# Two batches' router and the first weight splits in the projection's block, and VectorE instead of GpSimd for the last two normalisations

## The chip, the cores and the metric

One Trainium2 chip, one of its cores. The metric is the device time of one execution in microseconds (us), the median of several executions. Of the kernel before three are known: 793.04, 795.33 and 796.99 us, median 795.33 us.

## What is computed

Four blocks on x of 4 batches x 512 tokens x 256 features, all in float32, each with a layer norm ahead and a gated residual behind it:

```
x = x + tanh(g_xattn[0]) * attention(layernorm(x), ctx)      # 16 heads of 16, rotary, then @ Wp.T + bp
x = x + tanh(g_ffn[0])   * experts(layernorm(x))             # 8 experts, top 2, and a shared one
x = x + tanh(g_xattn[1]) * coattention(layernorm(x), ctx)
x = x + tanh(g_ffn[1])   * bitlinear_ffn(layernorm(x))
```

The expert block takes logits = xn @ gate_w.T + lb_bias, sigmoid scores, the two highest of eight per token, and one mean weight per expert over all tokens (so a routed expert's output needs the scores of all four batches). Each expert, and each half of the shared one, is silu(xn @ gw.T) * (xn @ uw.T) @ dw.T with 128 inner features.

## The kernel before, in words

Each phase is a function with a program of its own for each engine, in an order written out by hand. Engines meet at semaphores only, and all of them at the end of each phase. The phases are prepare (QKV), attend, project, experts, coattend and bitffn. Two of them are touched.

**Project** (`phase_project`). SyncE issues the load of Wp (L680) and then, from the list `loads` (L682), the experts' down and up weights and the later phases' context. For each batch b, in four groups of heads, ScalarE copies the attention sums to `stage` (L688), TensorE transposes them (`sums`, L718), VectorE divides by the softmax sums (`normalise`, L767 and L769). TensorE transposes the result (`transposes`, L726), ScalarE copies that (L693), TensorE multiplies by Wp (`project`, L737), and VectorE adds to x and takes the row statistics (`residual`, L780 and L786). TensorE's order is sums(b), project(b-1), transposes(b); VectorE's is normalise(b), residual(b-1). All but the first batches run in hardware loops (`Fori`). GpSimd normalises batches 0 to 2 for the experts (`normalise_batch`: `batch_statistics`, nine small operations from L172 to L184, then two passes over four tiles, L194 and L198).

**Experts** (`phase_experts`). GpSimd normalises batch 3. TensorE transposes the normalised rows of each batch (L882, 8 transposes), ScalarE copies them to `xT_all` (`keep`, L1002), and TensorE makes the router's logits from them (`router`, L889, 2 matmuls, 4 in the trace). In the order of TensorE these steps stand among the first matmuls of the shared expert:

```python
transposes(0); transposes(1); router(0); transposes(2); router(1)
gate_up(0, 0); router(2); transposes(3); router(3)
# transposes of the logits (L954), gate_up(0, 1), project(0, 0)
# transposes of the selection (L965), project(0, 1), gate_up(0, 2) ...
```

A matmul of the experts is the sum of three, of operands split in a high part (ScalarE rounds it: `high_w` L1010, `high_d` L1014, `high_x` L1006, `high_h` L1022) and the rest (VectorE subtracts: `low_w` L1097, `low_d` L1102, `low_x` L1107, `low_h` L1091). `gate_up(c, k)` is 12 matmuls (L902) for chunk c and expert k of the order, and a 13th for a routed expert, which adds a large negative number where a token has not chosen it; `project(c, k)` is 6 matmuls (L915 to L920). Between them ScalarE applies the silu (L1018) and VectorE multiplies (`hidden`, L1085). VectorE ranks the scores (L1156 to L1161); only then can TensorE transpose the selection (L965), and VectorE copies it (L1170).

Of the kernel before, what the change touches and what calls it, by code (L numbers as in the profile page):

```python
# [19 lines left out]
F32 = mybir.dt.float32  # L20
# [8 lines left out]
P = 128  # L29
# [172 lines left out]
def phase_prepare(nc, a, per, qs, ks, va):  # L202
# [4 lines left out]
    with ExitStack() as ctx:  # L207
        sb = lambda n, s, d: ctx.enter_context(nc.sbuf_tensor(n, s, d))
        ps = lambda n, s, d: ctx.enter_context(nc.psum_tensor(n, s, d))
        sem = lambda n: ctx.enter_context(nc.semaphore(n))  # L210
# [197 lines left out]
        def _(pe):  # L408
# [40 lines left out]
            schedule(pe, step)  # L449

# [12 lines left out]
def phase_attend(nc, a, per, qs, ks, va, o32):  # L463
    id32 = per["c32"][:, C_ID:C_ID + P]
    with ExitStack() as ctx:
# [189 lines left out]
def phase_project(nc, a, per, norm, qs, loads):  # L655
    x_sb, st = per["x"], per["st"]
    id32 = per["c32"][:, C_ID:C_ID + P]

    o32 = qs[:, :, :].rearrange("p h s -> p (h s)").bitcast(F32).rearrange("p (s c) -> p s c", s=STEPS)
    with ExitStack() as ctx:  # L660
# [11 lines left out]
        ps_y = [ps(f"ps_y{i}", [P, 2, D], F32) for i in range(2)]  # L672
        wp_in, staged, t_done, r_done, on_done = (sem("wp_in"), sem("staged"), sem("t_done"),
                                                         sem("r_done"), sem("on_done"))
        oT_done, oT_ready, y_done, y_used = sem("oT_done"), sem("oT_ready"), sem("y_done"), sem("y_used")
        block = ctx.enter_context(nc.Block())

        @block.sync
        def _(sp):
            sp.dma_start(wp[:, :, :], a["wp"]).then_inc(wp_in, 16)  # L680
            for dst, src, arrived in loads:
                sp.dma_start(dst, src).then_inc(arrived, 16)  # L682

        @block.scalar
        def _(act):
            def stage_sums(s, u):
                wait(act, t_done, s - 1)
                act.copy(stage[:, u, :], o32[:, ds(s, 1), 0:S].rearrange("p o c -> p (o c)")).then_inc(staged, 1)  # L688
# [6 lines left out]
            for g in range(NG):  # L695
                stage_sums(g, g % 2)
            stage_sums(NG, 0)
            stage_sums(NG + 1, 1)
            transposed(0)
            with act.Fori(1, B - 1) as b:  # L700
                stage_sums(b * NG + 2, 0)
                stage_sums(b * NG + 3, 1)
                stage_sums(b * NG + 4, 0)
                stage_sums(b * NG + 5, 1)
                transposed(b)
            stage_sums(STEPS - 2, 0)
            stage_sums(STEPS - 1, 1)
            transposed(B - 1)

        @block.tensor  # L710
        def _(pe):
            def sums(b, g):

                s = b * NG + g
                pe.wait_ge(staged, s + 1)
                wait(pe, on_done, s - 1)
                for qt in range(QT):
                    last = pe.transpose(ps_t[g % 2][:, qt, :, :].rearrange("p j c -> p (j c)"),  # L718
                                        stage[:, g % 2, qt * P:(qt + 1) * P], id32)
                last.then_inc(t_done, 1)  # L720
# [10 lines left out]
            def project(b):  # L731

                pe.wait_ge(oT_ready, b + 1)
                for qt in range(QT):
# [7 lines left out]
            for g in range(NG):  # L742
                sums(0, g)
            transposes(0)
            for g in range(NG):
                sums(1, g)
            project(0)
            transposes(1)
            with pe.Fori(2, B) as b:
                for g in range(NG):  # L750
                    sums(b, g)
                project(b - 1)
                transposes(b)
            project(B - 1)

        @block.gpsimd
        def _(pool):
            for b in range(B - 1):
                normalise_batch(pool, per, norm, b)

        @block.vector
        def _(dve):
            def normalise(b, g):
                s = b * NG + g
                dve.wait_ge(t_done, s + 1)
                wait(dve, on_done, s - NG + 1)
                dve.reciprocal(recip[:, g, :, :], ps_t[g % 2][:, :, :, HD]).then_inc(r_done, 1)  # L767
                dve.wait_ge(r_done, s + 1)
                dve.tensor_tensor(on[:, :, g * G * HD:(g + 1) * G * HD].rearrange("p q (j d) -> p q j d", d=HD),  # L769
                                  ps_t[g % 2][:, :, :, 0:HD],  # L770
                                  recip[:, g, :, :].rearrange("p q (j o) -> p q j o", o=1)
                                  .broadcast_to([P, QT, G, HD]), ALU.mult).then_inc(on_done, 1)

            def residual(b):
                for h in range(2):
                    k = b * 2 + h
                    dve.wait_ge(y_done, k + 1)
                    for q in range(2):
                        xs = x_sb[:, ds(b * QT + 2 * h + q, 1), :].rearrange("p o d -> p (o d)")
                        last = dve.scalar_tensor_tensor(out=xs, in0=ps_y[h][:, q, :],  # L780
                                                        scalar=coef[:, ds(b * QT + 2 * h + q, 1)],
                                                        in1=xs, op0=ALU.mult, op1=ALU.add)
                    last.then_inc(y_used, 1)
                    dve.wait_ge(y_used, k + 1)
                    for q in range(2):
                        dve.bn_stats(st[:, ds(b * QT + 2 * h + q, 1), :].rearrange("p o d -> p (o d)"),  # L786
                                     x_sb[:, ds(b * QT + 2 * h + q, 1), :].rearrange("p o d -> p (o d)"))\
                           .then_inc(norm["stats_done"], 1)
            for g in range(NG):
                normalise(0, g)  # L790
# [1156 lines left out]
```

## Time and profile before

| | |
|---|---|
| the profiled execution, its own time | 795.87 us |
| its span, first to last instruction | 794.0 us |
| busy in the span: TensorE / VectorE / ScalarE / GpSimd | 689.2 / 473.1 / 358.8 / 283.2 us |
| mean granted TensorE clock | 0.933 of full speed |
| attend ends, project begins | 307.9, 308.2 us |
| project ends, experts begins | 347.1, 347.5 us |

PE is TensorE's matmul (PEld its weight load), DVE VectorE, ACT ScalarE, POOL GpSimd, SP SyncE. A row of the timeline gives the start and the duration in us, the engine, the line, the operation, what it writes and reads and how often in a row, and in brackets the idle time before it and what ended that. A group of instructions gives count, busy us, mean ns of one, and the idle time before them.

### The profile page before, as it was taken

Reading aid. Unit: us, or ns where it says so; the run is one execution under the profiler, and the core shown is the slowest. Engines: PE = TensorE matmul, PEld = TensorE weight load, DVE = VectorE, ACT = ScalarE, POOL = GpSimd, SP = SyncE. Lnnn points to the kernel's source line nnn. Section 1 sums busy time; section 2 is a strip of 40 time slices with the busy share of each in tenths; the row PEclk is TensorE's granted clock in tenths of the full one; section 3 lists DMA queues with packets and bytes.
Section 4 is the critical chain, followed back from the end, with each engine's and each line's share of the span. In section 5 each row is a group of like instructions: output and inputs, shape, how many; then the busy total and the mean of one; then the engine's idle time right before and its main releaser. Section 6 shows DMA issues by size and latency. Waiting matters only on the chain. (4 is left out here: it accounts for less than half of the span.)

```text
span 794.0 us, 10607 instructions
## 1 busy us (share of the span) xinstructions
PE 689.2 (87%) x3503; PEld 441.0 (56%) x3522; DVE 473.1 (60%) x852; ACT 358.8 (45%) x644; POOL 283.2 (36%) x462
## 2 busy tenths in 40 slices
PE   3599959999999996878999999995699999966986
PEld 1277733433344333745777777774376776852554
DVE  3567658888888841746834343434355546447985
ACT  0156644888888886345432222431313031102665
POOL 1446523344433450580001010101040436246897
PEclk9799986999999999989999999998789899986999
DMA  6000000000000004800100000001100000000001
GB/s 195 14 27 26 20 8 0 1 1 1 1 1 1 1 1 164 314 15 0 70 37 1 1 0 0 1 0 43 25 1 0 1 1 0 1 0 2 26 33 47
DMA packets 14103, 21.43 MB, mean 27 GB/s; under 512 B 2161, under 2 KB 11505, under 8 KB 13297
## 3 DMA queue, kind: packets, MB, share of 16 engines
q1 hardware_dynamic: 13200, 20.34, 7.5%
q10 hardware_dynamic: 864, 0.59, 0.3%
q8 instruction: 23, 0.38, 0.2%
q14 instruction: 16, 0.12, 0.1%
HBM read 18.83 MB, written 2.10 MB: 26 GB/s over the span
## 5 line engine op out<-in xcount | busy, mean ns | idle before, releaser
L562 DVE TENSOR_REDUCE mx<-ps_f 128x2 f32<-128x1024 f32 x128 | 151.5, 1220 | 31.6 <-PE ps_f L500 31.3
L638 ACT ACTIVATE prob<-ps_s 128x512 f32<-128x512 f32 x256 | 134.6, 608 | 34.5 <-PE ps_s L518 34.5
L518 PE MATMUL ps_s<-q_stacks,k_stacks 64*128 64x512 f32 x256 | 90.2, 484 | 5.9 <-ACT prob L638 3.5
L518 PEld LDWEIGHTS ps_s<-q_stacks,k_stacks 64*128 64x128 f32 x256 | 35.8, 188 | 87.2 <-ACT prob L638 70.9
L500 PE MATMUL ps_f<-k_stacks,q_stacks 64*128 64x512 f32 x256 | 63.8, 449 | 6.8 <-DVE mx L562 5.3
L527 PE MATMUL ps_o<-prob,vst 128*32 128x512 f32 x512 | 69.0, 612 | 0.0
L1018 ACT ACTIVATE qs<-ps_g 128x512 f32<-128x512 f32 x40 | 23.9, 598 | 88.6 <-PE ps_u L902 88.6
L1085 DVE SCALAR_TENSOR_TENSOR h<-ps_u,most,qs 128x512 f32<-128x512 f32 x32 | 24.0, 751 | 62.5 <-ACT qs L1018 62.5
L589 POOL TENSOR_TENSOR q_stacks<-minus,q_stacks 128x1024 fp32r<-128x1024 f32 x16 | 38.0, 2372 | 55.0 <-ACT minus L629 55.0
L172 POOL TENSOR_TENSOR norm_tmp_att<-st 128x4 f32<-128x4 f32 x4 | 1.0, 240 | 142.4 <-DVE st L1124 142.4
L1527 ACT ACTIVATE qs<-ps_SC,nmax 128x512 f32<-128x512 f32 x16 | 11.0, 686 | 76.4 <-DVE nmax L1415 76.4
L1091 DVE TENSOR_TENSOR h_low<-h,h_high 128x512 fp32r<-128x512 f32 x40 | 27.6, 691 | 23.4 <-ACT h_high L1022 23.2
L1022 ACT CAST h_high<-h 128x512 fp32r<-128x512 f32 x40 | 24.8, 621 | 31.2 <-DVE h L1085 31.2
L500 PEld LDWEIGHTS ps_f<-k_stacks,q_stacks 64*128 64x128 f32 x256 | 30.8, 197 | 14.2 <-DVE mx L562 11.7
L393 POOL TENSOR_TENSOR qkr<-qkb,c 128x512 f32<-128x512 f32 x16 | 20.3, 1268 | 42.5 <-DVE stack L312 30.1
L1299 PE MATMUL ps_SC<-ks 128*128 128x512 f32 x64 | 31.8, 644 | 3.3 <-DVE ks L1409 2.3
L347 ACT CAST stack<-qkr 128x512 fp32r<-128x512 f32 x16 | 9.9, 618 | 54.0 <-DVE qkr L303 30.8
L430 PE MATMUL ps_kv<-wkv,ctxT 128*128 128x512 f32 x64 | 34.3, 663 | 0.0
L415 PE MATMUL ps_st<-c,stack 128*128 128x128 f32 x256 | 30.8, 274 | 3.9 <-ACT q_stacks L355 3.9
L1317 PE MATMUL ps_q<-ks,qs 128*128 128x256 f32 x128 | 30.9, 384 | 1.5 <-DVE hq L1444 1.5
L415 PEld LDWEIGHTS ps_st<-c,stack 128*128 128x128 f32 x256 | 28.7, 142 | 6.3 <-DVE stack L312 2.3
L916 PE MATMUL ps_yE<-h_high,down_low 128*128 128x512 f32 x80 | 32.1, 402 | 0.0
(278 smaller groups left out, 1524.2 us busy)
## 6 DMA issues: line engine op xcount, KB each, us to landing
up<-in_up SPq DMA_DIRECT2D x10, 256.0 KB, 6.7
x<-in_x SPq DMA_DIRECT2D x4, 512.0 KB, 8.0
ctxT<-in_ctxT SPq DMA_DIRECT2D x16, 128.0 KB, 2.1
ks<-in_ctxTC SPq DMA_DIRECT2D x1, 2048.0 KB, 13.3
ks<-in_ctx SPq DMA_DIRECT2D x1, 2048.0 KB, 18.8
out<-x SPq DMA_DIRECT2D x16, 128.0 KB, 1.7
down<-in_down SPq DMA_DIRECT2D x1, 1280.0 KB, 5.5
ks<-in_wqv SPq DMA_DIRECT2D x1, 1024.0 KB, 20.7
```

Of the source, the lines that this page charges most:

```text
L415: last = pe.transpose(ps_st[i][:, p, :], stack[:, u, i // 2, 2 * pair:2 * pair + 2, :] .rearrange("p h r -> p (h r)"), id32)
L430: last = pe.matmul(ps_kv[u][:, :, :], ctxT[:, u, c, :], wkv[:, c, :, :], start=(c == 0), stop=(c == DC - 1))
L500: last = pe.matmul(ps_f[n % 2][:, h, :], qs[rows(h), 2 * f + pair, qt * P:(qt + 1) * P], ks[rows(h), 2 * f + pair, :], start=True, stop=True)
L518: pe.matmul(ps_s[n % 3][:, :], ks[rows(h), 2 * s + pair, kt * P:(kt + 1) * P], qs[rows(h), 2 * s + pair, :], start=True, stop=True).then_i ...
L527: last = pe.matmul(ps_o[HPAD * j:HPAD * (j + 1), :], vst[:, s % 2, kt, HPAD * j:HPAD * (j + 1)], prob[:, kt % 2, j, :], start=(kt == 0), s ...
L562: dve.tensor_reduce(mx[:, f % 2, qt, 2 * pair:2 * pair + 2], ps_f[n % 2][:, :, :], AX_X, ALU.max).then_inc(used, 1)
L589: pool.tensor_tensor(own, minus[:, :, :].broadcast_to([P, 2, S]), own.bitcast(F32), ALU.add)\
L638: act.activation(prob[:, kt % 2, j, :], ps_s[n % 3][:, :], ACT.Exp, scale=SCALE)\
L916: pe.matmul(ps_y[half][:, :], down_low[:, e, own], h_high[:, u, :], start=False, stop=False)
L1091: dve.tensor_tensor(h_low[:, u, :], h32[:, u, :], h_high[:, u, :].bitcast(F32), ALU.subtract)\
L1299: last = pe.matmul(ps_S[q % 2][:, :], sT[:, c, q * P:(q + 1) * P], ctxT[:, c, ds(b * S, S)], start=(c == 0), stop=(c == DC - 1))
L1317: last = pe.matmul(ps_q[:, :], attT[:, q % 2, k, :], ctok[:, ds(b * QT + k, 1), :], start=(k == 0), stop=(k == QT - 1))
```

## The change

The PE, ACT and DVE loops of the projection are written out. In the projection's block, TensorE now also makes the router's logits of batches 0 and 1, the first of them between sums(3) and project(2), the second at the end, with one PSUM tile `ps_T` for the transposes. ScalarE and VectorE split the shared expert's weights in the loop over the batches, VectorE splits chunk 0 of x, normalises batch 2 itself (`normalise_late`, one pass of four tiles) and copies the first half of the logits. GpSimd takes only the statistics of batches 2 and 3. In the experts' block VectorE normalises batch 3, and the steps are reordered. gate_w is loaded by SyncE between Wp and the list `loads`. SyncE clears the first phase's semaphores in the attend phase, since more of them are needed now. The core of the diff:

```diff
@@ attend, SyncE
             sp.dma_start(bp[:, :], a["bp"].to_broadcast([P, D])).then_inc(bp_in, 16)
+            for done in spent:
+                sp.sem_clear(done)
@@ project, SyncE
             sp.dma_start(wp[:, :, :], a["wp"]).then_inc(wp_in, 16)
+            sp.wait_ge(gw_clear, 1)
+            sp.dma_start(gw[:, :, 0:E], a["gate_w"]).then_inc(gw_in, 16)
@@ project, ScalarE (was: the same order in a Fori, without the splits and keeps)
+            for s in range(NG + 2):
+                stage_sums(s)
+            for b in range(B - 1):
                 transposed(b)
+                for s in range(b * NG + 6, min(b * NG + 10, STEPS)):
+                    stage_sums(s)
+                if b == 1:
+                    act.wait_ge(pre["up_in"], 16 * (NX + 1))
+                    pre["high_w"](act, 0)
+                    pre["high_w"](act, 1)
+                    pre["high_d"](act, E, NX)
+            keep(0)
+            keep(1)
             transposed(B - 1)
+            pre["high_x"](act, 0)
+            for k in range(2, 4):
+                pre["high_w"](act, k)
+            keep(2)
+            keep(3)
@@ project, TensorE
+            def router(b):
+                pe.wait_ge(norm["normed"], b + 1)
+                for i in range(2):
+                    wait(pe, kept, 2 * b + i)
+                    for q in range(2):
+                        for c in range(DC):
+                            last = pe.transpose(ps_T[:, c, q * P:(q + 1) * P],
+                                                norm["tile"](b * QT + 2 * i + q)[:, c * P:(c + 1) * P], id32)
+                    last.then_inc(xT_done, 1)
+                if b == 0:
+                    pe.wait_ge(gw_in, 16)
+                pe.wait_ge(kept, 2 * b + 2)
+                for c in range(DC):
+                    last = pe.matmul(ps_lgT[HPAD * b:HPAD * (b + 1), :], gw[:, c, :], xT_all[:, c, b * S:(b + 1) * S],
+                                     start=(c == 0), stop=(c == DC - 1))
+                last.then_inc(lgT_done, 1)
+            sums(2)
+            project(1)
+            transposes(2)
+            sums(3)
+            router(0)
+            project(2)
+            transposes(3)
+            project(3)
+            router(1)
@@ project, GpSimd
-            for b in range(B - 1):
+            pool.memset(gw[:, :, :], 0.0).then_inc(gw_clear, 1)
+            for b in range(2):
                 normalise_batch(pool, per, norm, b)
+            for b in range(2, B):
+                batch_statistics(pool, per, norm, b)
@@ project, VectorE
+            normalise(0)
+            for b in range(1, B):
+                normalise(b)
                 residual(b - 1)
+                if b == 2:
+                    pre["low_w"](dve, 0)
+                    pre["low_w"](dve, 1)
+                    pre["low_d"](dve, 0, E, NX)
             residual(B - 1)
+            pre["low_x"](dve, 0)
+            normalise_late(dve, per, norm, 2, pre["late"])
+            dve.wait_ge(lgT_done, 2)
+            dve.tensor_copy(lgT[0:2 * HPAD, :], ps_lgT[0:2 * HPAD, :])
+def normalise_late(dve, per, norm, b, done):
+    x_sb, tmp = per["x"], norm["tmp"]
+    dve.wait_ge(norm["steps"], 5 * (b + 1))
+    for t in range(b * QT, (b + 1) * QT):
+        last = dve.tensor_scalar(norm["tile"](t), x_sb[:, t, :], tmp[:, 4, t:t + 1], tmp[:, 8, t:t + 1], ALU.add, ALU.mult)
+    last.then_inc(done, 1)
@@ experts, GpSimd: the memset of gw and normalise_batch(3) are gone
@@ experts, TensorE
-            transposes(0); router(0) ... (the order shown above)
+            pe.wait_ge(pre["late"], 1)
             transposes(2)
             pe.wait_ge(xsplit, 1)
+            pe.wait_ge(wsplit, 2)
+            gate_up(0, 0, (0,))
+            pe.wait_ge(pre["late"], 2)
+            transposes(3)
             router(2)
+            router(3)
+            gate_up(0, 0, (1,))
             pe.wait_ge(lgT_copied, 1)
...
             gate_up(0, 1)
             pe.wait_ge(nsel_ready, 1)
...
+            pe.wait_ge(lg_copied, 1)
+            pe.wait_ge(dsplit, 1)
+            project(0, 0)
             project(0, 1)
@@ experts, ScalarE
+            for k in range(4, 2 * B):
                 keep(k)
             act.wait_ge(lg_copied, 1)
             act.activation(score[:, :, :], logits[:, :, :], ACT.Sigmoid).then_inc(score_done, 1)
+            silu(0, 0)
+            pre["high_d"](act, 0, E // 2)
             silu(0, 1)
+            pre["high_d"](act, E // 2, E)
+            high_h(0, 0)
             high_h(0, 1)
             for k in range(SH, NX):
                 silu(0, k)
-                if k + 4 < NX:
-                    high_w(k + 4)
+                if k + 2 < NX:
+                    pre["high_w"](act, k + 2)
@@ experts, VectorE
+            normalise_late(dve, per, norm, 3, pre["late"])
             dve.tensor_copy(tri[:, :, :], c32[:, C_TRI:C_TRI + E * E].rearrange("p (e f) -> p e f", f=E))
+            pre["low_w"](dve, 2)
             dve.wait_ge(lgT_done, B)
+            dve.tensor_copy(lgT[2 * HPAD:P, :], ps_lgT[2 * HPAD:P, :]).then_inc(lgT_copied, 1)
... (logits)
+            pre["low_w"](dve, 3)
... (ranks)
+            hidden(0, 0)
             link(dve.tensor_tensor(weight, score[:, :, :], chosen, ALU.mult))
             hidden(0, 1)
... (the copies of the transposed selection)
+            low_h(0, 0)
             low_h(0, 1)
... (the mean weights)
-            low_d(1, 0, E // 2)
-            low_d(2, E // 2, E)
-            low_w(SH + 1)
+            pre["low_d"](dve, 1, 0, E // 2)
+            pre["low_d"](dve, 2, E // 2, E)
...
             for k in range(SH, NX):
                 hidden(0, k)
-                if k + 3 < NX:
-                    low_w(k + 3)
+                if k + 2 < NX:
+                    pre["low_w"](dve, k + 2)
```

## Rows read from the trace of the kernel before

**Rows 1.** Stretches: us, busy (count) of each engine, TensorE's granted clock, DMA share, GB/s
```profile
346.00:350.00 4.00, 2.52 (x11) 2.26 (x12) 0.80 (x2) 1.74 (x3) 3.37 (x14) 0.50 0.15 43
350.00:354.00 4.00, 4.00 (x14) 1.67 (x14) 2.78 (x3) 3.10 (x6) 3.88 (x4) 0.70 0.12 30
...
370.00:374.00 4.00, 1.90 (x15) 1.43 (x15) 3.80 (x7) 1.57 (x4) 0.00 (x0) 0.86 0.00 0
374.00:378.00 4.00, 4.00 (x19) 3.23 (x16) 3.46 (x9) 0.30 (x1) 0.00 (x0) 0.72 0.00 0
```

**Rows 2.** Timeline, the end of the projection and the start of the experts
```profile
340.35 0.20 POOL L172 TENSOR_TENSOR norm_tmp_moe<-st 128x4 f32<-128x4 f32 x1 [0.84 <-DVE st L786]
...
342.17 1.04 POOL L184 TENSOR_TENSOR norm_tmp_moe<-norm_tmp_moe,norm_power_moe 128x4 f32<-128x4 f32 x1
...
345.30 1.84 POOL L198 TENSOR_SCALAR qs<-qs,norm_tmp_moe 128x256 f32<-128x256 f32 x4
...
347.49 3.79 PE L882 MATMUL ps_xE<-c,qs 128*128 128x128 f32 x16 [3.98 <-PEq L660]
```

**Rows 3.** Timeline, VectorE: residual of batches 0, 1 and 3, and what follows
```profile
321.09 0.88 DVE L780 SCALAR_TENSOR_TENSOR x<-ps_y,coef,x 128x256 f32 x2 [1.09 <-PE ps_y L737]
...
324.98 0.26 DVE L767 RECIPROCAL recip<-ps_t 128x16 f32<-128x16 f32 x1
...
329.01 0.88 DVE L780 SCALAR_TENSOR_TENSOR x<-ps_y,coef,x 128x256 f32 x2 [1.07 <-PE ps_y L737]
...
332.62 0.26 DVE L767 RECIPROCAL recip<-ps_t 128x16 f32<-128x16 f32 x1
...
341.82 0.88 DVE L780 SCALAR_TENSOR_TENSOR x<-ps_y,coef,x 128x256 f32<-128x256 f32 x2 [1.55 <-PE ps_y L737]
...
344.45 0.75 DVE L786 BATCH_NORM_STATS2 st<-x 128x6 f32<-128x256 f32 x2
```

**Rows 4.** Timeline, TensorE's project(2) and project(3), and ScalarE between stages
```profile
331.02 1.07 ACT L693 COPY onT<-ps_oT 128x512 f32<-128x512 f32 x2 [3.18 <-PE ps_oT L726]
...
334.57 3.62 PE L737 MATMUL ps_y<-wp,onT 128*128 128x256 f32 x16
...
339.79 3.72 PE L737 MATMUL ps_y<-wp,onT 128*128 128x256 f32 x16 [0.73 <-ACT onT L693]
```

**Rows 5.** The page's DMA issues: KB each, median us from issue to landing
```profile
up<-in_up SPq DMA_DIRECT2D x10, 256.0 KB, 6.7
```

**Rows 6.** Group by shape, VectorE's splits of weights in the experts' phase
```profile
L1097 DVE TENSOR_TENSOR up_low<-up,w_high 128x512 fp32r<-128x512 f32 x8 | 5.5, 682 | 0.0
```

**Rows 7.** Timeline, the last batch's transposes and router, and the logits' transposes
```profile
361.27 1.09 PE L882 MATMUL ps_xE<-c,qs 128*128 128x128 f32 x8
...
361.96 1.07 ACT L1002 COPY qs<-ps_xE 128x512 f32<-128x512 f32 x2 [1.32 <-PE ps_xE L882]
...
363.09 1.90 PE L889 MATMUL ps_yE<-qs,gw 128*32 128x512 f32 x4 [0.73 <-ACT qs L1002]
...
365.11 0.69 DVE L1145 COPY qs<-ps_yE 128x512 f32<-128x512 f32 x1 [0.83 <-PE ps_yE L889]
...
365.85 0.66 PE L954 MATMUL ps_yE<-c,qs 128*128 128x128 f32 x4 [0.86 <-DVE qs L1145]
```

**Rows 8.** Single lines: ns min/median/max of one, first and last start
```profile
L280 DVE TENSOR_SCALAR xn<-x,meanA,rstdA x16: 404/406/1306, 10.0 to 88.1; 128x256 f32 x10, 128x256 f32<-128x256 f32 x6
...
L194 POOL TENSOR_SCALAR qs<-x,norm_tmp_moe x16: 473/478/1422, 328.1 to 354.3; 128x256 f32<-128x256 f32 x16
```

**Rows 9.** Timeline, from the selection's transposes to gate_up(0, 3)
```profile
372.80 1.88 PE L965 MATMUL ps_xE<-c,qs 128*128 128x128 bf16 x16 [2.10 <-DVE qs L1161]
...
375.01 1.28 DVE L1170 COPY nselT<-ps_xE 128x1024 bf16<-128x1024 bf16 x2
...
376.75 0.62 PE L902 MATMUL ps_g<-x_high,w_high 128*128 128x512 f32 x2
...
380.87 0.70 PE L902 MATMUL ps_g<-x_high,w_high 128*128 128x512 f32 x2 [0.84 <-DVE up_low L1097]
```

More of the change, by code:

```diff
@@ L741, in _ @@
             pe.wait_ge(wp_in, 16)
-            for g in range(NG):
-                sums(0, g)
+            sums(0)
             transposes(0)
-            for g in range(NG):
-                sums(1, g)
+            sums(1)
             project(0)
             transposes(1)
[L749 to L754, printed above, removed]
+            sums(2)
+            project(1)
@@ L762, in _, with normalise @@
         def _(dve):
[L763 to L772, printed above, removed]
+            def normalise(b):
+                for g in range(NG):
+                    s = b * NG + g
+                    dve.wait_ge(t_done, s + 1)
+                    wait(dve, on_done, s - NG + 1)
+                    if g == 0:
+                        wait(dve, oT_done, 2 * b)
+                    dve.reciprocal(recip[:, g, :, :], ps_t[g % 2][:, :, :, HD]).then_inc(r_done, 1)
+                    dve.wait_ge(r_done, s + 1)
+                    dve.tensor_tensor(on[:, :, g * G * HD:(g + 1) * G * HD].rearrange("p q (j d) -> p q j d", d=HD),
+                                      ps_t[g % 2][:, :, :, 0:HD],
+                                      recip[:, g, :, :].rearrange("p q (j o) -> p q j o", o=1)
+                                      .broadcast_to([P, QT, G, HD]), ALU.mult).then_inc(on_done, 1)
@@ L785, in residual @@
                     for q in range(2):
[L786 to L790, printed above, removed]
-            with dve.Fori(1, B) as b:
-                for g in range(NG):
-                    normalise(b, g)
+                        t = b * QT + 2 * h + q
@@ L801, in phase_experts @@
+def phase_experts(nc, a, per, norm, next_norm, pre, sg, h32, h_low, h_high, spare, nselT, up_low, down_low, w32, wabs,
+                  w32_in, abs_done):
     x_sb, c32, c16 = per["x"], per["c32"], per["c16"]
@@ L891, in router, with gate_up @@
                 last.then_inc(lgT_done, 1)
-            def gate_up(c, k):
+            def gate_up(c, k, halves=(0, 1)):
                 e, u = order[k], k % 2
@@ L898, in gate_up @@
                 terms = [(w, x, d) for w, x in terms for d in range(DC)]
-                for i, out in ((0, ps_g[u]), (1, ps_u[u])):
+                for i in halves:
+                    out = (ps_g[u], ps_u[u])[i]
                     masked = i == 0 and e < E
@@ L907, in gate_up @@
                         pe.matmul(out[:, :], skip[:, e, :], nselT[:, cols], start=False, stop=True)
-                last.then_inc(gu_done, 1)
+                if 1 in halves:
+                    last.then_inc(gu_done, 1)
             def project(c, k):
@@ L1171, in _ @@
                    .then_inc(nselT_ready, 1)
+            low_h(0, 0)
+            low_h(0, 1)
             link(dve.tensor_reduce(total[:, 0, :], weight, AX_X, ALU.add))
```

208 lines of the change are left out of this document (81 added, 127 removed).

## The prediction

> **What bounds the kernel now.** I read the table of engines first: TensorE is busy for 87% of the span, so time is lost only where it pauses or runs at its lower clock. The windows show where that is in the touched stretch: [rows 1] has the granted clock at 0.50 from 346 to 350 us and at 0.70 from 350 to 354, again below 1 from 370 to 378. The clock has two levels, 1.2 and 2.4 GHz, so 0.50 is the lower one throughout. Then the timeline gives the reasons. [rows 2]: TensorE has finished the projection at 343.5, but the block waits for GpSimd's normalisation of batch 2 until 347.14, and the experts begin at 347.49 on a slow array. Ahead of that, from 321 to 345 us, the projection is a ring: VectorE's residual, its normalise, TensorE's sums and project, the residual again [rows 3, 4]. Behind it the chain is TensorE, the ranks on VectorE, the selection's transposes at 372.80, and at 380.87 gate_up(0, 3) [rows 9]. From there TensorE has no pause of a whole microsecond, so what the change is worth is how much earlier gate_up(0, 3) starts.
>
> **The projection, step by step.** The sum is made against the profiled execution: 795.87 us, span 794.0, so 1.87 lie around it; it is 0.54 above the median of the runs.
>
> Loops written out: residual(0) and (1) last 3.89 and 3.61 us up to the next reciprocal, the unrolled residual(3) 344.45 + 0.75 - 341.82 = 3.38 [rows 3]. With 0.05 saved at each project ahead of them, both together bring 0.8: residual(1) ends at 331.8.
>
> New on VectorE there: two weight splits and one of down, all of 512 columns, 0.68 each [rows 6], 2.05 us in front of normalise(3), whose first operation starts at 333.9 instead of 332.62. Nothing hides them: sums(3) of the third group waits for it. ScalarE's halves (three copies, some 1.9 us) fit into its pause of 3.18 us [rows 4]; without it they would delay the copy for project(2). Their weights were issued by 314 us and land 6.7 us later [rows 5], ahead of their use at 327. The gate_w load moves `down` and `up` back by its own issue, some 0.5 us, with 6 us to spare, and Wp stands ahead of it. Clearing semaphores falls on SyncE, idle in attend: nothing.
>
> router(0) stands between sums(3) and project(2), in TensorE's own order. With one PSUM tile a half is 0.69 us from the first transpose to ScalarE's copy, 0.59 the copy, 0.06 back; twice that is 2.68, and the four matmul passes are 1.90 [rows 7]: 4.6 us, uncovered. GpSimd has normalised batch 0 before that. project(2) started 1.95 after normalise(3) began (334.57 - 332.62), so now at 333.9 + 1.95 + 4.6 = 340.45. project(3) follows 5.2 later [rows 4], at 345.65; residual(3) runs from 347.7 to 351.05; router(1) starts 3.6 after project(3), takes 4.6 and ends at 353.85; the copy of its logits 0.12 + 0.69 more [rows 7], to 354.7. Beside it VectorE has low_x(0) (1.36, two of [rows 6]) and four tiles of batch 2 at 0.41 [rows 8], done at 354.05. keep and high copies of ScalarE lie beside these.
>
> GpSimd's statistics of batch 3 take 2.86 us (340.35 to 342.17 + 1.04 [rows 2]), from 351.15 to 354.0, if nothing holds them. But VectorE subtracts and scales from SBUF at that very time, and rows show that each can hold the other: L280 took 1.306 instead of 0.406 us, L194 1.422 instead of 0.478 [rows 8]. Bounds of the delay: nothing, or low_x plus four tiles, 1.36 + 1.64 = 3.0, which would end the block at 357. The small operations have waits between them in which VectorE's can pass, so I take 1.5: statistics at 355.5, block at 355.5, 0.8 beyond 354.7. The Trainium skill (SBUF — State Buffer, SBUF: two separate sides) makes this an exclusive lock, in which the loser is held for the other's whole instruction. By that rule in full the sum would be 1.5 higher than mine; L194's row has such a hold of one operation.
>
> **The experts, step by step.** Begin at 355.5 + 0.3 = 355.8, 8.3 later than 347.49. Left for TensorE until the logits' transposes end: 1.1 transposes(2), 1.4 half of gate_up, 1.1 transposes(3), two routers 3.8, half of gate_up 1.4, 0.66 [rows 7]: 9.5, so 365.3 against 365.85 + 0.66 = 366.5 before: 1.2 gained. VectorE normalises batch 3 in 1.65, ready at 357.5, before TensorE asks at 358.3; its copy of the logits lies under the second half of gate_up.
>
> From there to gate_up(0, 3) it was 380.87 - 366.5 = 14.4. Now: low_w(3) stands before the ranks and is 0.68, where VectorE had a pause of 0.38 for the sigmoid: selection's transposes after 6.3 + 0.3 = 6.6, done at 8.5. project(0, 0) used to lie in the pause ahead of them and now lies behind. VectorE has hidden(0, 0), hidden(0, 1), 1.28 for the selection and low_h(0, 0) (2.75 us with the small ones) from 6.8 to 10.5; until then project(0, 0) can't end. Its last two passes 0.5, project(0, 1) 1.5, gate_up(0, 2) and the sums 3.3: 15.8. The wait of 0.84 for up_low [rows 9] is gone, since low_w(3) is done. That is 1.4 worse: the gain is given back, and gate_up(0, 3) starts at 381.1, 0.2 later than before. Later pairs of steps stay TensorE's.
>
> Clock: the new pause ahead of sums(3)'s third group is 2.8 us (331.8 to 334.6), and TensorE idles 3.6 instead of 2.1 us before the selection's transposes. After a pause of 2.1 us the rows have the low level for 0.14 x 2 x 4 + 0.28 x 2 x 4 = 3.4 us [rows 1], half of it lost. Bounds for each place: nothing, or 1.7; the cold start after 347.49 is gone in the step sum above. I take 0.5 in all, as much of the stretch waits for VectorE anyway.
>
> Sum: 0.2 + 0.5 on the execution's 795.87, that is 796.6, and on the median 795.33 + 0.7 = **796.0 us**.
>
> **Rivals.** (1) Slower, by the clock. Place: the splits in front of normalise(3). If the pause drops the array to 1.2 GHz as that at 343.5 did, where it stayed low for 4.0 + 2.4 = 6.4 us [rows 1], router(0) and project(2) lose up to 3.2, and the longer pause before the selection 1.7. 795.5 (the sum without a clock term) + 3.2 + 1.7 = 800.4. It decides from about 3 us of lower level in busy time. For it: 2.1 us were enough once; against it: the slices of the page show full clock through the projection's batches, which have pauses of 1 to 1.5 us. The Trainium skill (TensorE: Matmul & The Clock Gate, What's actually happening) has the array throttled by default and released by activity, which speaks against adding pauses. 0.18. (2) The hold between GpSimd and VectorE at its full 3.0 us: 796.0 + 1.5 = 797.5, still no change in a measurement. 0.14, where nothing else goes wrong. (3) Faster: VectorE's splits find slack in the ring, no hold, no low clock, and project(0, 0) overlaps the selection better: 795.5 - 2.05 - 0.8 (the hold) - 1.5 = 791.2. Against it: sums(3) waits for VectorE in every batch. 0.15. (4) The change doesn't do what it says: all orders are by hand, so nothing can put the steps elsewhere; no chance given.
>
> **Numbers.** No change as summed 0.53, with (2) 0.67; slower 0.18; faster 0.15. A measurement here tells apart about 0.5%, 4 us. The range from 791 to 800.5 takes in both ends of the unknown costs and leaves some 0.2 outside. The likeliest case alone is 793.5 to 798.5.
>
> **What would show it.** Right: the projection's block ends near 355.5 with GpSimd's statistics last, the logits' transposes end near 365, gate_up(0, 3) starts at 380 to 382, TensorE waits some 3.6 us for the selection. Wrong: router(0) costing well under 4.6, normalise(3) starting before 333, low clock from 334 to 341, or a start of gate_up(0, 3) outside 378 to 384.

## The result and the profile after

The median after is 797.22 us (793.07 to 799.08), beside 794.80 us (792.79 to 796.99) of the kernel before: a ratio of 1.003, 95% interval 1.0019 to 1.0042. That is 2.4 us slower and less than the 0.5% named ahead: no change in the sense of the forecast, 1.2 us above its number. The interval doesn't hold 1, though, so the small loss is real, and it is larger than the 0.7 us that the sum had forecast. The profiled execution took 798.58 us with a span of 796.8; the one before had 795.87 and 794.0.

The page of the kernel after, its totals of TensorE and the granted clock over 40 slices:

```profile
PE 692.7 (87%) x3503; PEld 443.0 (56%) x3522; DVE 475.9 (60%) x861; ACT 357.4 (45%) x643; POOL 276.3 (35%) x446
PEclk9699986999999999997999999998689899986999
```

The share of TensorE is still 87%. A page can't show where 2.4 us went, so I read the same stretch as before. Its measure in all that follows is the time from the issue of Wp, the first of the projection's block, to the start of gate_up(0, 3). Before, that is 308.15 to 380.87 = 72.72 us. After, it is 307.73 to 383.11 = 75.38, or 2.66 more. Outside the stretch the two traces differ by 0.14 us (308.15 + 413.13 before, 307.73 + 413.69 after). So near an agreement is partly chance: over the fourteen traces of this study the part ahead of the stretch takes 305.4 to 309.6 us and the part behind it 409.9 to 414.1, in code that the edits leave alone. The stretch itself repeats far better, 75.38 and 75.43 in two executions of the changed kernel.

The timeline of the kernel after, from residual(1)'s end to project(2) (start, duration, engine, line, operation, count, and in brackets the idle time ahead and what ended it), which answers to [rows 3, 4]:

```profile
330.92 1.28 DVE L876 TENSOR_TENSOR up_low<-up,w_high_shared 128x512 fp32r<-128x512 f32 x2
332.12 0.68 DVE L885 TENSOR_TENSOR down_low<-down,d_high_shared 128x512 fp32r<-128x512 f32 x1
332.72 0.25 DVE L815 RECIPROCAL recip<-ps_t 128x16 f32<-128x16 f32 x1
...
333.57 1.25 PE L741 MATMUL ps_t<-c,stage 128*128 128x128 f32 x8 [2.53 <-DVE on L817]
...
334.66 0.98 PE L772 MATMUL ps_TP<-c,qs 128*128 128x128 f32 x4
...
338.20 3.54 PE L779 MATMUL ps_lgTP<-qs,gw 128*32 128x512 f32 x4 [0.77 <-ACT qs L712]
...
341.67 3.72 PE L760 MATMUL ps_y<-wp,onT 128*128 128x256 f32 x16
```

The three splits stand between residual(1) and normalise(3), and TensorE's pause behind them is 2.53 us. Then router(0) runs from 334.66 to 341.67, 7.0 us instead of the 4.6 of the sum. Its four matmul passes take 3.54 us, and 1.90 for router(1) later in the same block: the lower of the two levels of TensorE's clock. The windows of the kernel after (first the stretch and its length, then each engine's busy time with its count, the granted clock, the DMA share and GB/s), which answer to [rows 1]:

```profile
334.00:338.00 4.00, 2.76 (x14) 1.79 (x12) 1.31 (x5) 1.11 (x2) 3.70 (x8) 0.59 0.07 27
338.00:342.00 4.00, 3.80 (x6) 0.84 (x7) 0.00 (x0) 0.06 (x1) 1.14 (x3) 0.56 0.02 4
342.00:346.00 4.00, 4.00 (x24) 3.57 (x22) 2.20 (x6) 0.14 (x1) 0.00 (x0) 1.00 0.00 0
...
358.00:362.00 4.00, 4.00 (x18) 3.39 (x16) 1.39 (x5) 1.24 (x3) 0.00 (x0) 0.58 0.24 67
...
374.00:378.00 4.00, 3.99 (x19) 2.98 (x17) 3.94 (x8) 1.24 (x2) 0.00 (x0) 0.50 0.00 0
378.00:382.00 4.00, 4.00 (x15) 3.02 (x16) 3.41 (x6) 0.00 (x0) 0.00 (x0) 0.86 0.01 4
```

There are three low stretches in these rows, and each follows a pause of TensorE: 2.53 us ahead of 334, 2.43 at the start of the experts, 3.63 ahead of the selection. Now the end of the projection's block, with GpSimd's statistics of batch 3 (the timeline of the kernel after, which answers to [rows 2]):

```profile
352.33 1.21 DVE L894 TENSOR_TENSOR x_low<-qs,x_high 128x1024 fp32r<-128x1024 f32 x1
352.56 1.03 POOL L172 TENSOR_TENSOR norm_tmp_moe<-st 128x4 f32<-128x4 f32 x1 [2.52 <-DVE st L834]
353.45 1.38 DVE L854 TENSOR_SCALAR qs<-x,norm_tmp_moe 128x256 f32<-128x256 f32 x4
...
355.10 0.68 DVE L847 COPY lgT<-ps_lgTP 64x512 f32<-64x512 f32 x1 [0.27 <-PE ps_lgTP L779]
...
355.74 1.04 POOL L184 TENSOR_TENSOR norm_tmp_moe<-norm_tmp_moe,norm_power_moe 128x4 f32<-128x4 f32 x1
...
357.49 1.07 PE L975 MATMUL ps_xE<-c,qs 128*128 128x128 f32 x8 [2.43 <-PEq L668]
```

The statistics last from 352.56 to 356.78, 4.2 us instead of 2.86 [rows 2]; the block waits for them, a whole microsecond after the copy of the logits, and the experts begin at 357.49. The rest of the chain in the same timeline, which answers to [rows 7, 9]:

```profile
366.42 0.60 PE L1043 MATMUL ps_yE<-c,lgT 128*128 128x128 f32 x4
...
373.43 1.89 PE L1050 MATMUL ps_xE<-c,qs 128*128 128x128 bf16 x16 [3.63 <-DVE qs L1202]
...
379.98 0.63 PE L996 MATMUL ps_g<-x_high,w_high 128*128 128x512 f32 x2
...
383.11 0.70 PE L996 MATMUL ps_g<-x_high,w_high 128*128 128x512 f32 x2
```

Cut at the start of the experts and at the end of the logits' transposes, the stretch is 39.34 + 19.02 + 14.36 = 72.72 us before and 49.76 + 9.53 + 16.09 = 75.38 after. The projection's part grew by 10.42, the experts' first part lost 9.49, and the part behind the logits grew by 1.73.

### The profile page after: what moved, and what is told of

Its sections match the earlier page's. It is cut to its first block and busy times, and to the rows that moved or that the text cites. A ratio compares the mean times of both kernels' runs of the same rounds, so it can differ in the third digit from the quotient of the medians.

```text
span 796.8 us, 10544 instructions
## 1 busy us (share of the span) xinstructions
PE 692.7 (87%) x3503; PEld 443.0 (56%) x3522; DVE 475.9 (60%) x861; ACT 357.4 (45%) x643; POOL 276.3 (35%) x446
## 5 line engine op out<-in xcount | busy, mean ns | idle before, releaser
L172 POOL TENSOR_TENSOR norm_tmp_att<-st 128x4 f32<-128x4 f32 x4 | 1.0, 241 | 144.6 <-DVE st L1169 144.6
```

## The experiments

Theory A, after the result: the splits' place costs their own 2.05 us and, through the pause, the lower clock in router(0), about 2.4 more. B: the clock has nothing to do with that pause, and router(0) is slow in this place for another reason. Later runs went after the hold of GpSimd, the order behind the logits, and the single parts of the change. The expectations compare with the kernel after unless they say otherwise. There are twelve runs, eleven new kernels and the change itself again. The last column is measured side by side with the kernel before and is not always the quotient of two medians:

| kernel | stretch, us | median, us (runs) | ratio to before, 95% |
|---|---|---|---|
| before | 72.72 | 794.80 (20) | |
| after | 75.38 | 797.22 (20) | 1.0030, 1.0019 to 1.0042 |
| e1, splits later | 70.73 | 791.86 (7) | 0.9951, 0.9935 to 0.9968 |
| e2, filled pause | 73.96 | 795.18 (12) | 0.9994, 0.9976 to 1.0011 |
| e3, router(0) at the end | 71.72 | 794.28 (10) | 0.9974, 0.9958 to 0.9990 |
| e4, loops alone | 71.58 | 792.85 (10) | 0.9945, 0.9923 to 0.9967 |
| e5, e1 and low_x ahead | 68.49 | 790.77 (4) | 0.9942, 0.9925 to 0.9958 |
| e6, e1 and filled rank pause | 68.62 | 791.68 (4) | 0.9949, 0.9931 to 0.9967 |
| e7, e1 and project ahead | 70.55 | 789.95 (4) | 0.9933, 0.9916 to 0.9950 |
| e8, normalisation alone | 74.88 | 796.57 (10) | 1.0017, 0.9995 to 1.0039 |
| e9, e5 and e7 | 67.90 | 787.25 (4) | 0.9911, 0.9877 to 0.9945 |
| e10, e9 and filler | 66.79 | 788.82 (4) | 0.9918, 0.9902 to 0.9935 |
| e11, e5 and filler | 67.72 | 789.16 (4) | 0.9920, 0.9900 to 0.9941 |
| e12, the change again | 75.43 | 797.21 (6) | 1.0025, 1.0012 to 1.0038 |

The ratio is to the runs of the kernel before on the same chip, whose median moved between 794.7 and 796.4.

A stretch is one execution's, and its sum hides where the clock was low. So it is cut here as above, at the start of the experts and at the end of the logits' transposes:

| kernel | projection | experts' first part | behind the logits |
|---|---|---|---|
| before | 39.34 | 19.02 | 14.36 |
| after | 49.76 | 9.53 | 16.09 |
| e12 | 49.82 | 9.53 | 16.08 |
| e1 | 45.45 | 7.99 | 17.29 |
| e2 | 47.29 | 9.58 | 17.09 |
| e3 | 47.52 | 7.99 | 16.21 |
| e4 | 37.69 | 19.53 | 14.36 |
| e5 | 44.30 | 7.99 | 16.20 |
| e6 | 45.40 | 8.00 | 15.22 |
| e7 | 46.48 | 9.52 | 14.55 |
| e8 | 40.91 | 19.61 | 14.36 |
| e9 | 44.51 | 7.99 | 15.40 |
| e10 | 44.26 | 7.99 | 14.54 |
| e11 | 44.52 | 7.99 | 15.21 |

In the kernels that have the change's order, the first part takes 8.0 us where the clock stays at 1.00 and 9.5 where it falls. No edit touches that part.

### The splits in another place (e1)

```diff
                 normalise(b)
-                residual(b - 1)
-                if b == 2:
+                if b == 3:
                     pre["low_w"](dve, 0)
                     pre["low_w"](dve, 1)
                     pre["low_d"](dve, 0, E, NX)
+                residual(b - 1)
```

> The changed kernel with the three splits of VectorE moved from ahead of normalise(3) to behind it, into the 8 us in which VectorE waits for project(2). Clock theory (the splits open a pause of 2.8 us on TensorE, after which it falls to 1.2 GHz and router(0) takes 7.0 instead of 4.6 us): both go, 2.05 + 2.4, project(2) starts 4.4 us earlier relative to the block's start and the median is about 793. Work theory (the slow router is not the pause's doing): only the 2.05 go, router(0) still takes about 7 us, about 795.

The timeline of e1, TensorE alone:

```profile
331.75 1.25 PE L741 MATMUL ps_t<-c,stage 128*128 128x128 f32 x8 [0.72 <-DVE on L817]
332.84 0.60 PE L772 MATMUL ps_TP<-c,qs 128*128 128x128 f32 x4
...
335.54 1.88 PE L779 MATMUL ps_lgTP<-qs,gw 128*32 128x512 f32 x4 [0.77 <-ACT qs L712]
337.35 3.72 PE L760 MATMUL ps_y<-wp,onT 128*128 128x256 f32 x16
...
353.14 1.06 PE L975 MATMUL ps_xE<-c,qs 128*128 128x128 f32 x8 [2.40 <-PEq L668]
```

With the pause at 0.72 us, router(0) takes 337.35 - 332.84 = 4.5 us, and project(2) starts 4.3 us earlier than in the kernel after, at the same issue of Wp within 0.04 us. 1.8 of these are the third group's earlier start, 2.5 the shorter router(0). The stretch falls by 4.65 us and the kernel becomes 0.5% faster than before. Only the 4.3 are the edit's: the experts' first part is 1.5 shorter, since behind the same pause (2.40 us) the clock stayed high this time, and the part behind the logits is 1.2 longer. Moving three operations of VectorE by one step of its ring is worth more than the whole change loses; that the 2.5 are the clock's, e1 alone can't show.

### The pause kept but filled (e2)

```diff
+                    if s == STEPS - 3:
+                        for i in range(18):
+                            pe.transpose(ps_T[:, i % 2, 0:P], id32, id32)
```

The transposes of a constant are work on top, between the second and the third group of sums(3); the splits stay where the change put them.

> The changed kernel with 18 more transposes of a constant on TensorE in the pause ahead of the third group of sums(3), some 2.4 us of work into an unused PSUM tile; nothing waits for them and all orders stay. Clock theory: the clock holds at 1.00 from 334 to 342, router(0) takes 4.6 us, about 2.4 us faster than the changed kernel, near 794.8. Work theory: no faster than the changed kernel, 797.

The timeline of e2, TensorE alone, and one of its windows:

```profile
329.89 2.13 PE L746 MATMUL ps_TP<-c 128*128 128x128 f32 x18
332.60 1.25 PE L741 MATMUL ps_t<-c,stage 128*128 128x128 f32 x8 [0.57 <-DVE on L820]
333.68 0.60 PE L775 MATMUL ps_TP<-c,qs 128*128 128x128 f32 x4
...
338.19 3.72 PE L763 MATMUL ps_y<-wp,onT 128*128 128x256 f32 x16
```
```profile
354.00:358.00 4.00, 4.00 (x16) 3.50 (x17) 1.91 (x6) 1.17 (x2) 0.00 (x0) 0.58 0.19 67
```

This settles it between A and B. The third group still starts where VectorE lets it, 332.60 - 306.68 = 25.9 us after the issue of Wp (after: 25.8), and router(0) takes 4.5 us instead of 7.0. So 2.5 us of the kernel after are the clock's alone, set off by the pause. Only 1.4 of them stay in the stretch: the experts start at the lower clock here as in the kernel after (0.58), and the part behind the logits is 1 us longer. The time agrees with the trace: 0.9994 of before against 1.0030 for the kernel after, with intervals apart, though this kernel does more work.

### Both routers behind project(3) (e3)

```diff
@@ TensorE
-            router(0)
             project(2)
...
             project(3)
+            router(0)
             router(1)
```

ScalarE's two copies for router(0) move behind its copy for project(3).

> The changed kernel with router(0) behind project(3), next to router(1), and ScalarE's two copies behind the copy for project(3). The same work on TensorE. If router(0) costs what it does because it stands in the ring, residual(3) comes 7 us earlier, GpSimd's statistics of batch 3 are done under the routers and the block ends about 1.7 us earlier: near 795.5. If the place doesn't matter, TensorE's sum is the same and only the hold of the statistics (1.1 us) goes: near 796.1.

The timeline of e3, TensorE alone:

```profile
333.04 1.25 PE L741 MATMUL ps_t<-c,stage 128*128 128x128 f32 x8 [2.53 <-DVE on L817]
334.13 5.30 PE L760 MATMUL ps_y<-wp,onT 128*128 128x256 f32 x16
```

The pause is the same 2.53 us, and now project(2) pays for it, 5.30 instead of 3.72 us. The stretch is 3.7 us shorter than after. 2.2 of them lie in the projection, for two reasons that this run doesn't part: the low clock costs 1.6 instead of 2.5, and router(0) lies beside the last residual and the statistics of batch 3 instead of in front of them. The other 1.5 are the experts' first part at the full clock, behind a pause of 1.17 us instead of 2.43.

### The parts of the change by themselves (e4, e8)

e4 is the kernel before with its three projection loops written out (TensorE's is shown, ScalarE's and VectorE's are alike):

```diff
-            with pe.Fori(2, B) as b:
+            for b in range(2, B):
```

> The kernel before with nothing but the projection's loops of TensorE, ScalarE and VectorE written out. By the step sum 0.8 us, 0.1% faster than before, near 794.0, to be seen in the trace as project(3) starting 30.9 instead of 31.6 us after the block's first instruction. If the unrolled code costs elsewhere (instruction loads): no gain or slower.

The stretch is 1.1 us shorter, against 0.8 in the sum. At project(3), where the expectation looked, it is 1.3: it starts 335.76 - 305.43 = 30.3 us after the issue of Wp, 31.6 before. The time is lower by more than that, 0.55% by the ratio and 3.6 us between the medians: in the profiled execution the issue of Wp itself came 2.7 us earlier, in phases that the edit does not touch. Why they ran faster stays open.

e8 is the kernel before with the other part alone: GpSimd makes the statistics of batches 2 and 3 in the projection's block, and VectorE scales them.

```diff
-            for b in range(B - 1):
+            for b in range(2):
                 normalise_batch(pool, per, norm, b)
+            for b in range(2, B):
+                batch_statistics(pool, per, norm, b)
... (VectorE's normalise_late(2) behind residual(3), its normalise_late(3) first in the experts)
```

> The kernel before with nothing but the normalisation of batches 2 and 3 by VectorE (one pass of four tiles each, statistics still on GpSimd, those of batch 3 in the projection's block). By the step sum the block ends about 0.5 us earlier or up to 1.5 later, as GpSimd's statistics of batch 3 run beside VectorE's four tiles, 345.2 + 2.9 to 4.2 against 347.1 before; TensorE did not wait for batch 3 later. So no gain, 0 to 2 us slower in the stretch. If the two slow passes of GpSimd bounded the experts' start, 1.5 us faster or more.

The timeline of e8:

```profile
343.33 0.22 POOL L172 TENSOR_TENSOR norm_tmp_moe<-st 128x4 f32<-128x4 f32 x1 [2.15 <-DVE st L796]
...
345.53 1.04 POOL L184 TENSOR_TENSOR norm_tmp_moe<-norm_tmp_moe,norm_power_moe 128x4 f32<-128x4 f32 x1
...
347.10 2.30 PE L892 MATMUL ps_xE<-c,qs 128*128 128x128 f32 x9 [5.62 <-PEq L668]
```

The experts begin 347.10 - 306.19 = 40.9 us after the issue of Wp, 1.6 later than before: the scaling left GpSimd, but the statistics of batch 3, 3.24 us behind the last residual, came into the block in its place. They can't start earlier, since they need that residual. The stretch is 2.2 us longer, 0.6 of it in the experts' first part. In time this part alone is worth nothing, 1.0017 with 1 inside the interval.

### The subtraction away from GpSimd's statistics (e5)

e1 and:

```diff
+            pre["low_x"](dve, 0)
             residual(B - 1)
-            pre["low_x"](dve, 0)
```

> The kernel of e1_splits_later with low_x(0) ahead of residual(3), in VectorE's pause for project(3), so that it no longer runs beside GpSimd's statistics of batch 3. Hold theory (an operation of GpSimd that reads SBUF waits for VectorE's whole subtraction: L172 took 1.04 instead of 0.20 us): the statistics take 0.8 to 1.0 us less than their 4.2, and the projection's block, which they end, is that much shorter. If the stretched rows are the profiler's and GpSimd is only slow: the 4.2 us stay and the block ends as in e1.

The timeline of e5, GpSimd alone:

```profile
349.95 0.23 POOL L172 TENSOR_TENSOR norm_tmp_moe<-st 128x4 f32<-128x4 f32 x1 [1.45 <-DVE st L834]
...
352.16 1.04 POOL L184 TENSOR_TENSOR norm_tmp_moe<-norm_tmp_moe,norm_power_moe 128x4 f32<-128x4 f32 x1
```

and TensorE's first row of the experts:

```profile
353.87 1.06 PE L975 MATMUL ps_xE<-c,qs 128*128 128x128 f32 x8 [1.43 <-PEq L668]
```

L172 takes 0.23 us here, and 1.03 in the kernel after beside low_x (1.04 in e1). The statistics take 3.25 us instead of 4.2, and the experts begin 353.87 - 309.57 = 44.30 us after the issue of Wp instead of e1's 45.45. So 1.0 of the 1.4 us by which the statistics were held came from that one subtraction; the other 0.4 also show in e8, whose statistics have only the four tiles of scaling beside them (3.24 us). The stretch is 2.2 us shorter than e1's, 1.1 of it behind the logits, where this edit changes nothing and e1 happened to be slow; the ratios, 0.9942 and 0.9951, lie inside each other's intervals and don't part the two kernels.

### The rank pause filled (e6)

e1 and 26 transposes of a constant behind gate_up(0, 1), again work on top:

```diff
+            for i in range(26):
+                pe.transpose(ps_x[0][:, i % 2, 0:P], id32, id32)
```

> The kernel of e1_splits_later with 26 more transposes of a constant on TensorE in its pause of 3.6 us before the selection's transposes. If the low clock behind that pause costs time: the clock stays at 1.00, the selection's transposes take 1.1 us and project(0, 0) and (0, 1) some 1.5 us less in all, and the matmul of the sums comes 1.0 to 1.5 us earlier. If VectorE's chain (copies of the selection, low_h) sets the pace there: under 0.5 us.

The timeline of e6, TensorE alone:

```profile
362.47 3.00 PE L1047 MATMUL ps_xE<-c 128*128 128x128 f32 x26
366.25 1.07 PE L1052 MATMUL ps_xE<-c,qs 128*128 128x128 bf16 x16 [0.78 <-DVE qs L1204]
...
369.97 0.73 PE L1015 MATMUL ps_yE<-h_low,d_high_shared 128*128 128x512 f32 x2 [0.90 <-DVE h_low L1154]
```

The granted clock is 1.00 from 314 to 382, and from the start of the logits' transposes to the sums' matmul it is 15.68 us instead of 17.75 in e1: 2.1 us less. Against e1, whose low stretch behind this pause was a long one, the filler looks worth too much; between e5 and e11, or e9 and e10 below, it is 1.0. Of a faster TensorE a part turns into a wait for VectorE's low_h, 0.90 us. In time it can't be told from e1 (0.9949 and 0.9951).

### project(0, 0) ahead of the selection again (e7)

e1 and, in short: TensorE makes the main passes of project(0, 0) ahead of its wait for the ranks, as the kernel before did, and VectorE and ScalarE bring hidden(0, 0) and high_h(0, 0) forward.

```diff
+            project(0, 0, (0,))
...
-            project(0, 0)
+            project(0, 0, (1,))
```

> The kernel of e1_splits_later with the first four matmuls of project(0, 0) in TensorE's pause before the selection's transposes, hidden(0, 0) among VectorE's rank operations and low_h(0, 0) right behind the selection. Theory that the change gives its gain back by having put project(0, 0) behind the selection: the matmul of the sums comes about 1.2 us earlier, although the selection is 0.7 us later. If the place of project(0, 0) doesn't matter: the same, or 0.7 later.

The timeline of e7, TensorE alone:

```profile
363.57 0.60 PE L1046 MATMUL ps_yE<-c,lgT 128*128 128x128 f32 x4
...
369.81 0.77 PE L1011 MATMUL ps_yE<-h_high,d_high_shared 128*128 128x512 f32 x1 [2.86 <-ACT h_high L1102]
...
378.46 0.29 PE L1065 MATMUL ps_xE<-sums,ones 128*128 128x16 f32 x2
```

From the logits' transposes to the sums it is 14.89 us, 2.9 less than in e1 and more than the 1.2 expected. Most of that isn't the order's: the windows from 370 to 378 have the clock at 0.64 and 1.00 here, and at 0.50 and 0.79 in e1. The order itself comes out of e9 and e10 below as 0.8. The stretch as a whole is only 0.2 shorter than e1's, since the clock was low twice where e1's was not: the block began at the lower level (0.50 from 314 to 318, where e1 had 0.97), 1.0 us, and the experts' start fell (0.73 and 0.85 from 354 to 362), 1.5 us. The ratio is 0.9933 to e1's 0.9951, and the intervals overlap.

### Together (e9, e10, e11) and the change again (e12)

e9 has the edits of e5 and e7, e10 adds 22 transposes of a constant behind gate_up(0, 1), e11 is e5 with the 26 of e6.

> The kernel of e1_splits_later with the edits of e5_low_x_earlier and e7_project_first together. If the two gains lie behind one another (0.9 us in the projection's block, 1.5 to 2.5 us from the logits' transposes on), gate_up(0, 3) starts 68 us after the first issue of the projection's block, against 70.7 in e1, and the time is 0.8% under the kernel before. If each only moves the other's wait: as e1 or e5.

> The kernel of e9_both_orders with 22 transposes of a constant on TensorE between gate_up(0, 1) and the first matmuls of project(0, 0). If what is left behind that pause is the low clock: the clock stays at 1.00 and gate_up(0, 3) starts another 0.5 to 1.0 us earlier. If it is VectorE's chain: no change.

> The kernel of e5_low_x_earlier with the filled pause of e6_filled_rank_pause, orders otherwise those of the change. Clock theory: 1 us or more under e5, near e10, since the low level behind that pause was worth as much as the order. Order theory: near e5, 1.5 us over e9.

> The changed kernel unaltered, on this chip and beside these runs. Both theories: 0.2 to 0.4% slower than the kernel before, low clock somewhere between sums(3) and project(2).

The timeline of e9, TensorE alone:

```profile
357.88 0.60 PE L1046 MATMUL ps_yE<-c,lgT 128*128 128x128 f32 x4
...
365.96 1.93 PE L1056 MATMUL ps_xE<-c,qs 128*128 128x128 bf16 x16
...
373.74 0.29 PE L1065 MATMUL ps_xE<-sums,ones 128*128 128x16 f32 x2
```

and that of e10:

```profile
359.69 0.60 PE L1046 MATMUL ps_yE<-c,lgT 128*128 128x128 f32 x4
...
362.91 2.56 PE L1050 MATMUL ps_xE<-c 128*128 128x128 f32 x22
...
374.59 0.29 PE L1067 MATMUL ps_xE<-sums,ones 128*128 128x16 f32 x2
```

e9 is the fastest kernel of the study by its median, 787.25 us, 0.9911 of before and below both kernels. Its transposes of the selection still run at the lower clock (1.93 us for 16; e6 has 1.07). e10 takes that away and its stretch is the shortest, 66.79, but its time can't be told from that of e9, nor can e11's. So the fillers of the rank pause have shown themselves in the trace and not beyond that.

These runs part the order from the clock. From the start of the logits' transposes to the sums' matmul it is:

| | without filler, clock low | with filler, clock at 1.00 |
|---|---|---|
| the change's order | e5: 16.66 | e11: 15.67 |
| project(0, 0) ahead | e9: 15.86 | e10: 14.90 |

The order is worth 0.8 us at either level of the clock, and the clock 1.0 us in either order. The expectation of e9 held (67.9 for 68 us, 0.9% under before), and so did the clock's side of that of e10 (1.1 us earlier). For e11 neither theory fits: its stretch is 0.8 under e5 and 0.9 over e10, as both the clock and the order count.

e12 is the change unaltered, to see whether its low stretches are its own. The timeline, TensorE alone:

```profile
333.75 1.29 PE L741 MATMUL ps_t<-c,stage 128*128 128x128 f32 x8 [2.52 <-DVE on L817]
334.84 1.06 PE L772 MATMUL ps_TP<-c,qs 128*128 128x128 f32 x4
...
338.46 3.46 PE L779 MATMUL ps_lgTP<-qs,gw 128*32 128x512 f32 x4 [0.77 <-ACT qs L712]
341.85 3.50 PE L760 MATMUL ps_y<-wp,onT 128*128 128x256 f32 x15
```

The same pause, the same slow router(0), 7.0 us; the same ratio.

## Why the prediction was right, and where it was not

The verdict and the range held, and the time, at 797.2 against 796.0. The difference it forecast did not: 0.7 us slower, measured 2.4. And of its own signs of being wrong one appeared, the low clock from 334 to 341. Two more were near: normalise(3) starts at 332.72, which is 333.1 counted from the same issue of Wp, against the limit of 333, and gate_up(0, 3) at 383.11 lies behind the 380 to 382 that it called right. So the number is good partly by luck, as the steps show. By its steps, with times after the issue of Wp (308.15 in the sum, 307.73 here):

- **Splits ahead of normalise(3).** Predicted 2.05 us, hidden by nothing. The rows show 1.28 + 0.68 and the third group waiting 2.53 for VectorE, and in e1, without them, that group starts 1.8 us earlier. normalise(3) begins at 25.0 us instead of 25.75: residual(1) was done earlier than the sum had it. The loops, 0.8 in the sum, measured 1.3 at project(3) in e4.
- **router(0) in the ring.** Placed rightly, with 4.6 us; at full clock it is 4.5 (e1, e2, and router(1) here, 350.55 to 355.05). It took 7.0. **This is the term that was mis-sized:** the clock stood with 0.5 us for both places, and it cost 2.5 at this one (e2), and 1.5 at a third place that the sum took as gone, the experts' start (9.53 against e1's 7.99). At the selection the whole low stretch is worth 1.0 (e5 beside e11, e9 beside e10), and the kernel before had a part of that too. Rival 1 named the place and a price of up to 3.2 us, and it acted there, though not with its total of 800.4 us. I gave it little for the full clock of the slices in pauses of 1 to 1.5 us; those rows said nothing about one of 2.5. The sentence of the Trainium skill (TensorE: Matmul & The Clock Gate, What's actually happening) that the array is throttled by default and released by activity was the one that pointed the right way, and e2 agrees: activity without any use, in the same pause, kept the clock at 1.00.
- **project(2).** Predicted 32.3 us after the issue, measured 33.9.
- **GpSimd's statistics.** Predicted 2.86 + 1.5 us, last in the block; measured 4.2, last in the block. e5 shows the subtraction's part, 1.0. From the statistics' end to the experts' start it is 0.7 instead of 0.3. The rule of the Trainium skill (SBUF — State Buffer, SBUF: two separate sides), the loser held for the other's whole instruction, is stated there for VectorE operations with two inputs from SBUF or in a two-port mode, which the prediction left out. The trace agrees for the subtraction, which has two inputs: L172 took 1.03 beside its 1.21. The bound of 3.0, in which every VectorE operation holds GpSimd in full, did not come: beside the scaling three small operations took 0.37 to 0.39 and the others 0.20 to 0.24.
- **The experts' first part.** Predicted 9.5 us at full clock, measured 9.53, but with a low stretch in it (0.58 from 358 to 362). At full clock it is 361.13 - 353.14 = 8.0 (e1). Two errors cancelled: the step was 1.5 too long, and the clock filled it. Most of the 1.5 are the two routers, summed as twice 1.9: back to back their eight passes take 2.70 us (e1). That the cold start of before "is gone" did not hold: the block still ends with a pause of 2.43 us.
- **Behind the logits.** Predicted 15.8 us, 1.4 worse than before; measured 16.1, 1.7 worse. The wait for the selection is 3.63 us, as forecast. The gain was given back here. The place of project(0, 0) accounts for 0.8 us of it (e5 beside e9, e11 beside e10). The other 0.9 no run parts: low_w(3) ahead of the ranks is among it, and the clock is low for longer behind the longer pause, by the windows some 6.9 us here against 3.4 before [rows 1].
- **gate_up(0, 3).** Predicted 72.95 us after the issue, without the 0.5 for the clock; measured 75.38. It is 2.4 late, and router(0)'s clock alone is 2.5. The other errors, up to 1.5 us each, cancel, and that is the luck in the number. The statement that TensorE has no pause of a whole microsecond from there on holds for the experts' block only (0.84 at most); later ones are up to 10.4 us (L1288, 10.6 after), and none of them took the delay up.

Against the kernel before, the change loses about what the clock takes in router(0). The +2.4 us of the time and +2.66 of the stretch agree; that nothing outside it changed rests on this and on the 0.14 us between two traces, where such parts move by 4 us from execution to execution. The rivals of a full hold and of a gain did not come: a full hold would have made the statistics 1.6 us longer than they were, and for a gain normalise(3) would have had to begin without the splits' time.

## What to carry to other kernels

Work that is put into a ring should stand where another engine's wait covers it, and a chain of engines should be priced with the pause that it opens on TensorE: here 2 us of VectorE cost 4.3, more than half of it through the clock. An edit that gains 1 us at one place can be given back at the next wait, so each later edge of the chain (statistics, ranks, h_low) has to be costed too; the kernel with the lowest median has three orders changed together. And two traces that differ in a clock level somewhere can't be compared as wholes: e7 beside e1 made an order of 0.8 us look like 2.9, and only a pair at the same level showed its worth. And of steps that must follow the last result, here the statistics, only their companions can be moved.

## What the runs showed of the hardware

- A pause of about 2.5 us in a stretch where TensorE is sparsely busy put its clock to the lower level for some 7 us (0.59 and 0.56 in the windows from 334 to 342), twice at the same place (after, e12). In e3, with project(2) instead of router(0) behind the pause, it was low for about half as long (0.57 from 334 to 338, 1.00 from there). 2.1 us of transposes of a constant in that pause kept it at 1.00 (e2). Pauses of 2.40 to 2.43 us at the start of the experts did this in after, e2, e7 and e12, and not in e1 and e6, so the pause alone doesn't decide; what does stays open. Pauses of 1.17 to 1.43 us at the same place did it in no run (e3, e5, e9, e10, e11).
- GpSimd's operation on 128x4 (L172) took 0.20 us alone [rows 2] and 1.03 beside VectorE's subtraction of 1.21 us; beside VectorE's scaling of 0.35 us a tile two or three of the operations that followed took 0.36 to 0.39 where they take 0.20 to 0.23 alone (after, e5, e8).
- VectorE's scaling of a 128x256 tile is 1.38 us for four back to back, 0.345 each, where GpSimd's row has 0.473 [rows 8].
- Eight router passes of two batches back to back took 2.70 us at the full clock (e1), where four take 1.90.
- TensorE's filler took nothing from its neighbours that the rows show: 18 transposes in 2.13 us, and the third group started at the same time after the issue.
